# VectorE's order inside one tile of a two-layer transformer: the last outputs of tile u-2 later, the second low heads of tile u earlier

## The reference

```
# layer 0
y = layernorm(x) * (1 + gamma1) + beta1            # per sequence, from cond
x = x + alpha1 * (attention(y) @ proj_w + proj_b)
z = layernorm(x) * (1 + gamma2) + beta2
x = x + alpha2 * (gelu(z @ fc1_w + fc1_b) @ fc2_w + fc2_b)
# layer 1: the same shape of layer with rotary q and k, a mask, no gates (alpha = 1)
```

## Time and profile before

| | |
|---|---|
| median of 3 runs | 1880.49 us (1879.55 to 1880.6) |
| the profiled execution | 1880.13 us, of which the traced span is 1878.3 us |
| PE busy | 1787.6 us (95%) |
| PE loading weights | 1636.5 us (87%) |
| DVE busy | 1236.8 us (66%) |
| ACT busy | 1306.6 us (70%) |
| POOL busy | 850.8 us (45%) |
| DMA engines, mean busy share | 39.9% |
| granted TensorE clock, mean | 0.988 of full |
| chain that ended last | PE 73%, DVE 12%, issue 8%, ACT 3% |

### The profile page before, as it was taken

How to read it: one execution, slowest core, us unless ns; L and a number is a source line. 1 busy time by engine, 2 the same in 40 slices (tenths; PEclk the granted TensorE clock), 3 DMA queues, 4 the chain that set the end, 5 groups by cost and what they waited for, 6 DMA issues and landing times.

```text
span 1878.3 us, 41749 instructions
## 1 busy us (share of the span) xinstructions
PE 1787.6 (95%) x12623; PEld 1636.5 (87%) x12623; DVE 1236.8 (66%) x2985; ACT 1306.6 (70%) x2327; POOL 850.8 (45%) x1036
## 2 busy tenths in 40 slices
PE   6689999999999999999899999999999999999998
PEld 5578888888898888898789989999999999999986
DVE  6577666767666766765867657667666766666751
ACT  4356776777777777777677776776776677777663
POOL 2123333343333334333356655556565555566534
PEclk8889999999999999999999999999999999999999
DMA  6545333544433444444454323333323333333320
GB/s 158 133 103 129 98 99 99 131 120 128 104 101 93 126 120 126 113 99 128 119 154 110 86 88 103 98 107 110 89 85 108 98 101 106 106 85 94 94 71 34
DMA packets 330275, 199.84 MB, mean 106 GB/s; under 512 B 160994, under 2 KB 314596, under 8 KB 330212
## 3 DMA queue, kind: packets, MB, share of 16 engines
q1 hardware_dynamic: 330212, 199.06, 39.9%
HBM read 80.98 MB, written 17.33 MB: 52 GB/s over the span
## 4 chain that ended last, share of the span: by engine, by line
PE 73%; DVE 12%; issue 8%; ACT 3%; SPq 1%; POOL 1%; DMA 1%; DVEq 0%; POOLq 0%; ACTq 0%
PE D L1145 17%; PE C L954 16%; PE B L954 9%; PE B L1101 8%; PE A L1068 7%; PE A L954 5%; PE B L1087 5%; PE E L954 4%; DVE mx L1415 2%; DVE o_sb L1439 2%; PE A L1073 2%; DVE exps L1421 1%; DVE ot_lo L1448 1%; PE E L1112 1%; ACT hact L773 1%
## 5 line engine op out<-in xcount | busy, mean ns | idle before, releaser
L583 POOL TENSOR_TENSOR h_lo<-hact,h_hi 128x512 fp32r<-128x512 f32 x256 | 330.3, 1290 | 310.7 <-ACT h_hi L778 297.6
L1068 PE MATMUL A<-k_pad,q_pad 128*128 128x256 f32 x1536 | 260.2, 297 | 19.0 <-DVE exps L1421 9.3
L1145 PE MATMUL D<-wgt_hi,h_hi 128*128 128x256 f32 x1024 | 263.5, 290 | 0.0
L787 ACT COPY probs_turned<-B 128x512 f32<-128x512 f32 x256 | 147.7, 584 | 166.2 <-PE B L1087 166.2
L1101 PE MATMUL B<-v_blocks,probs_turned 128*128 128x68 f32 x2048 | 255.8, 272 | 1.4 <-ACT probs_turned L787 1.4
L1101 PEld LDWEIGHTS B<-v_blocks,probs_turned 128*128 128x128 f32 x2048 | 250.4, 193 | 6.7 <-ACT probs_turned L787 2.4
L1145 PE MATMUL D<-wgt_lo,h_hi 128*128 128x256 f32 x1024 | 255.7, 282 | 0.0
L773 ACT ACTIVATE hact<-C,b_col 128x512 f32<-128x512 f32 x256 | 176.1, 688 | 98.7 <-PE C L954 95.9
L1068 PEld LDWEIGHTS A<-k_pad,q_pad 128*128 128x128 f32 x1536 | 215.1, 195 | 22.7 <-issue 11.7
L1415 DVE TENSOR_REDUCE mx<-A 128x8 f32<-128x512 f32 x256 | 173.9, 679 | 72.6 <-PE A L1073 40.3
L782 ACT ACTIVATE exps<-exps 128x512 f32<-128x512 f32 x256 | 160.9, 630 | 70.6 <-DVE exps L1421 69.8
(11 more groups left out here) (141 smaller groups left out, 3941.6 us busy)
## 6 DMA issues: line engine op xcount, KB each, us to landing
k_pad<-k_flat SPq DMA_DIRECT2D x512, 64.0 KB, 2.1
q_pad<-q_flat SPq DMA_DIRECT2D x256, 128.0 KB, 2.3
gates<-gates SPq DMA_DIRECT2D x64, 256.0 KB, 4.5
x_bias<-x_bias SPq DMA_DIRECT2D x32, 512.0 KB, 3.4
rotation<-rotation SPq DMA_DIRECT2D x256, 64.0 KB, 1.9
x_in<-in_x SPq DMA_DIRECT2D x16, 512.0 KB, 4.2
gates<-gated_bias SPq DMA_DIRECT2D x32, 256.0 KB, 4.6
x_res<-in_x SPq DMA_DIRECT2D x16, 512.0 KB, 4.2
```

The costliest lines, as they stand in the source:

```text
L583: pool.tensor_tensor(hb[1][:, m % 2, :], hact[:, m % 2, :], hb[0][:, m % 2, :].bitcast(F32), ALU.subtract).then_inc(h_lo, 1)
L1068: ins = nc.tensor.matmul(dst, qpad[g % 2][:, c, p, b, :, :].rearrange("p x s -> p (x s)"), kpad[g % 2][:, c, q, :, b * S:(b + 1) * S], sta ...
L1145: ins = nc.tensor.matmul(Dk[g // 2][:, (g % 2) * D:(g % 2 + 1) * D], hb[p][:, m % 2, g * P:(g + 1) * P], w_slice(q, W_FF2, D, m, 0, D), st ...
```

## The change

Only the order of calls in DVE's `step` changes; no instruction is added or removed, and the other engines' programs are the same. Before, DVE did both gated halves and both outputs of tile u-2 (in layer 1 the second output) in one piece ahead of group 1's first reciprocals. Now the second half's gate goes behind `normalise_heads(u, 1, 1)`, the first output of layer 0 behind `residual(u, b, 0)`, and the second output, in both layers, behind `low_heads(u, b, 1)`. That `low_heads` itself moves ahead of `second_statistics(u, 0)`, `y_scale(u+1, 0)` and `second_aggregate(u, 0)`, and `gate_heads(u, 1)` moves ahead of `y_shift(u+1, 0)` and `y_scale(u+1, 1)`.

```diff
@@ -1536,11 +1536,6 @@
                     output(u - 2, p, 0)
                 if c is not None:
                     z_low(u - 1, 1)
-                if p == 0:
-                    gate_output(u - 2, 1)
-                    output(u - 2, p, 0)
-                if p is not None:
-                    output(u - 2, p, 1)
                 if b is not None:
                     reciprocals(u, 1, 0)
                     maximum(u, 2, 0)
@@ -1550,23 +1545,30 @@
                     reciprocals(u, 1, 1)
                     subtract(u, 2, 0)
                     normalise_heads(u, 1, 1)
+                if p == 0:
+                    gate_output(u - 2, 1)
                 if b == 0:
                     gate_heads(u, 0)
                 if b is not None:
                     residual(u, b, 0)
+                if p == 0:
+                    output(u - 2, p, 0)
+                if b is not None:
                     subtract(u, 2, 1)
+                    low_heads(u, b, 1)
+                if p is not None:
+                    output(u - 2, p, 1)
+                if b is not None:
                     second_statistics(u, 0)
                 if a is not None:
                     y_scale(u + 1, 0)
                 if b is not None:
                     second_aggregate(u, 0)
-                    low_heads(u, b, 1)
+                if b == 0:
+                    gate_heads(u, 1)
                 if a is not None:
                     y_shift(u + 1, 0)
                     y_scale(u + 1, 1)
-                if b == 0:
-                    gate_heads(u, 1)
-                if a is not None:
                     y_shift(u + 1, 1)
```

## The result

The changed kernel takes **1885.78 us** (median of 8 runs, 1882.4 to 1888.21); the kernel before took 1879.57 on the same chip (8 runs, 1877.26 to 1881.05). The ratio is 1.0034, 95% interval 1.0025 to 1.0043: slower by about 6.2 us, above the 0.2% that can be told from no change.

The account below looks back on a forecast made before the run. PE was taken to bound the kernel, so time is won only where it waits. Terms 2.9 + 0.8 + 1.0 - 0.5 = +4.2 against the profiled 1880.13, rounded down to 1884.0 us; own range 1881 to 1887, wider range 1879 to 1889.

Parts of the forecast that it names:

- step 16: Change of layers: second output delays SP's feed-forward weights, then swaps and first high k; +1.0 us (-1.3 to +4).
- The gain: Layer-0 steps: DVE reaches group 1's low heads sooner, so PE's projection 1 starts earlier; 0.75 us per step won.
- What becomes late: Layer-0 steps 1 to 15: late aggregate and nb delay ACT's second copy; net +0.19 us per step, +2.9 in all.
- The rule on the DRAIN: DVE: a flush after every operation would make order free, costing 0.9 us, not 2.9; the trace disagreed by 0.13.
- Layer 1: Layer-1 steps: aggregate and second_norm come 0.6 to 0.9 us later with 0.9 of room; cost 0 (0 to +0.1).
- Step 0: First step: the second gate ahead of y_shift makes y_low late for PE; +1.0 us, of which 0.8 kept.
- Step 17: PE's wait of 0.62 us for the first low heads shrinks; -0.5 us.
- The other steps' SP queue: SP's store, gate2, x1m copy, x_in and gated bias come 6 us later outside step 16; costed at nothing.
- Nothing is forgiven: Rival: full delay per layer-0 step, 0.35 us, and weights cost 3 or 4 at the layer change; 1888.7 us, chance 0.20.
- the q chain: DVE and ACT chain to group 3's low q: forecast moves it 0.28 less 0.08 to 0.10 us; a rival, all 0.28.
- The lead is kept: Rival: ACT's second_norm isn't the late one, so 0.75 us per layer-0 step stays won; 1869 us, chance 0.15.

Follow-up runs that it names:

- Experiments 4: Changed kernel, with DVE's second_statistics(u, 1) ahead of y_low(u+1, 0) and second_aggregate(u, 1) ahead of y_low(u+1, 1); 1880.4 us, ratio 1.0010.
- Experiment 5: Changed kernel, DVE untouched, with ACT's second_norm(u, 1) behind exponential(u, 2, 1) instead of ahead of it; 1881.14 us, ratio 1.0009.
- experiment 6: Kernel before, with only low_heads(u, b, 1) and gate_heads(u, 1) moved as in the change, gated half and outputs left in place; 1881.75 us, ratio 1.0019.
- experiment 7: Changed kernel, with low_heads(u, b, 1) and gate_heads(u, 1) back in their old places, so only gated half and outputs moved; 1901.72 us, ratio 1.0121.
- experiment 3: Changed kernel, with SP loading the gated bias behind the swaps of tile 16 in step 15 alone; 1884.03 us, ratio 1.0029.
- 8: Changed kernel with three repairs: earlier group-1 aggregate, gated bias behind step 15's swaps, feed-forward weights ahead of step 16's store; 1872.88 us, ratio 0.9972.
- experiment 11: Changed kernel with three repairs, DVE's first layer-0 residual ahead of the second gated half, and ACT's second_norm(u, 1) behind move_probs(u, 2, 1); 1869.33 us, ratio 0.9953.
- experiment 1: Changed kernel, with steps 15 and 16 keeping DVE's order of before; 1880.5 us, ratio 1.0010.
- experiment 2: Changed kernel, with SP issuing layer 1's two feed-forward weights ahead of its wait for the second output in step 16; 1882.57 us, ratio 1.0025.
- experiment 9: Kernel before with three repairs (earlier aggregate, gated bias behind step 15's swaps, weights first in step 16) and nothing of the change; 1878.15 us, ratio 0.9996.

## Why the prediction was right in part

The range of 1879 to 1889 held the time, and so did the forecast's own, 1881 to 1887. The forecast of 1884.0 was 1.8 low and on the wrong side of the 0.2%: within had 0.45, slower 0.40. That it came so near is in part luck: step 16 was put 2.9 too low and step 15's queue at nothing, while the plain steps were put 0.9 too high and some 1.2 that came back behind step 16 was put at 0.5.

**The gain** was right to 0.02 in each place. Less the shift of 1.61 it put DVE's first normalise of group 1 at 508.82 (measured 508.82), PE's wait for x_res at nearly 1 (0.86), projection 1 0.75 earlier (0.76).

**What becomes late** was right in mechanism and nearly in size: aggregate at 521.02 (520.98), second_norm at 522.99 (522.94), ACT's wait about 0.5 (0.57), second copy at 528.16 (528.10). The term was +0.19 per step; measured +0.13. The term was mis-sized by 0.06: 15 x 0.13 = 2.0 in place of 2.9. Experiments 4 and 5 show the link that was only argued: remove the late nb, or let ACT work on past it, and 0.32 to 0.36 per step of the lead of 0.75 stays.

**The rule on the DRAIN.** y_shift of the second pair starts 0.73 behind the y_scale it depends on (517.79, 518.52), and that y_scale starts 0.60 behind the y_shift of the first pair (517.19), on which it doesn't depend. The aggregate came where the 0.73 puts it. The section The DRAIN you can't avoid in the Trainium skill, VectorE: DVE Perf Modes, says that a semaphore between two operations costs nothing extra; in the new order the trace again disagrees, by the 0.13. The prediction read the section too narrowly, though: it also says that a next operation that is not held starts earlier, and so doesn't by itself make the order free.

**Layer 1**: 0 expected; 0.00 to 0.08 less per step in steps 19 to 29. Right there. Step 30 is 0.23 shorter, with the low heads moved alone (experiment 6) too; why stays open. The reason was only half read: experiment 7 shows that layer 1 does react when the output stands ahead of late low heads.

**Step 0**: y_lo is late for PE by 3.47 in place of 2.13, 1.34 more, in the place named. The prediction had 1.0 by a slip: 65.71 plus its own 2.6 is 68.3, not "near 68.0", which gives the 1.34. What that costs in the end can't be told from the variation of the start-up.

**Step 17** was put at -0.5; it is 0.1 shorter. The waits of 0.62 and 0.29 for ot_lo are gone there, and one of 0.44 for x_res has come.

**Step 16** was named with its place (the second output, SP, the weights, the swaps, the high k), with a landing at 990.3 and the high k at 990 to 992; measured 991.1 and 993.3, of which 0.85 is the step's later start. The step that failed is "I take +1.0 for step 16 in place of the -1.3 (from -1.3, if the weights get out of the way, to +4)", a value for which the prediction gives no working: it was 3.9, since the delay of the k reached PE with two waits and a stretch of slower clock behind them. From the rows, the waits are 3.0, the clock is about 1.6 (0.29 of 5.6 us, an estimate), and the waits for ot_lo that are gone (1.60 and 0.29, against a new 0.44 for x_res) give back 1.45: 3.2, and 0.7 stays unplaced. The time came at the upper end of its own bounds.

**The other steps' SP queue** failed in one place: "I cost it at nothing" holds for steps 2 to 13 (experiments 4 and 5 keep SP as late as the change does, and their plain steps are shorter than before), but the sentence covered step 15 too, where the swaps of layer 1's first tile stand in the same queue behind the gated bias. It cost 0.6 to 1.9 (experiment 3 against the changed kernel, and 8 against 4).

**The rivals.** "Nothing is forgiven" (1888.7) had the weights right at 3 or 4 and the q chain wrong. "The lead is kept" (1869) was not what the change did. Experiment 5 keeps half of the lead (0.36 of 0.75 per step) and experiment 11 0.54; that the latter came out at 1869.33 is luck of the number, since it has further edits.

## What to carry to other kernels

When operations are moved on one engine, follow each semaphore they raise into every queue that waits for it, and look at the steps where those queues hold something extra: two irregular steps, 15 and 16 of 32, carried three quarters of this loss by the medians of experiment 1, and plain steps gave no sign of it. A result that comes late costs only through what is queued behind its reader, so where an in-order engine blocks on it, letting that reader stand two instructions later can be worth as much as making the result earlier. And test the halves of a reordering apart and together: here both halves lose alone, the whole loses through three side effects, and the whole without them wins.

## What the runs showed of the hardware

- 64 KB transfers issued from 982.29 on, 1 us behind two of 1024 KB, were used only at 991.90, 9.6 us later (the swaps of step 16; their median to landing is 1.9), while the DMA engines moved 332 GB/s. The same transfers at the same place in the step, with the large ones 16 us ahead (experiment 2), were not late.
- Two idle stretches of PE, 1.69 and 1.33 us with 0.74 us of work between, were followed by a granted clock of 0.71 over 5.6 us. In experiments 3 and 4, with 1.81 and 0.93 and with 2.34 and 0.84, it was 0.79 over 16 us (0.89 in the changed kernel), and step 16 was 0.9 longer still. A wait of PE costs more than its length there.
- The same code can be granted different clocks: behind PE's 5 to 6 us of idle time at the border of steps 14 and 15 the clock over 12 us was 0.86 in the profile of the kernel before and 0.72 in that of experiment 9, which has the outputs in the same places, and the two steps took 119.83 and 120.89. One profile of each kernel can't settle a difference of 1 us behind such a stretch.
- Steps of plain code repeat to 0.05 us, so a change of 0.1 us per step is read from one trace, where whole runs of one kernel, varying by 2 to 7 us, need many.
